# Last layer of a four-layer gated graph network: the state copied beneath the edge sums, part of the low h moved, the new state behind the n gate's argument

## The reference

```python
for l in range(4):
    m = x @ weight[l]
    agg = segment_sum(m[src], dst, num_segments=50000)
    gi = agg @ w_ih.T + b_ih              # i_r, i_z, i_n
    gh = x @ w_hh.T + b_hh                # h_r, h_z, h_n
    r = sigmoid(i_r + h_r); z = sigmoid(i_z + h_z)
    n = tanh(i_n + r * h_n)
    x = (1 - z) * n + z * x
return layernorm(input + (x + input), eps=1e-5)
```

## Time and profile before

| | |
|---|---|
| Median of three runs | 2331.55 us (2330.46 to 2332.36) |
| Span of the profiled execution (first to last instruction) | 2327.4 us |
| Busy in the span | TensorE 96%, VectorE 93%, ScalarE 79%, GpSimd 74% |
| Granted TensorE clock, mean | 0.986 |

### The profile page before, as it was taken

How to read it: one execution, slowest core, us unless ns; L and a number is a source line. 1 busy time by engine, 2 the same in 40 slices (tenths; PEclk the granted TensorE clock), 3 DMA queues, 4 the chain that set the end, 5 groups by cost and what they waited for, 6 DMA issues and landing times.

```text
span 2327.4 us, 49180 instructions
## 1 busy us (share of the span) xinstructions
PE 2229.5 (96%) x11728; PEld 1898.3 (82%) x11728; DVE 2175.6 (93%) x4211; ACT 1842.3 (79%) x3483; POOL 1719.4 (74%) x1654
## 2 busy tenths in 40 slices
PE   3999999999999999999999999999989999999996
PEld 2888888888878888888878888888877888888885
DVE  7899999999879999999969999999969999999998
ACT  1688888888768888888857888888856888888886
POOL 3877777777487777777558777777748888888884
PEclk7999999999999999999999999999999999999998
DMA  2455555555545555555545555555544555555554
GB/s 58 120 155 160 158 160 161 158 160 160 157 131 173 171 173 172 174 172 173 166 127 172 172 171 172 173 174 171 174 130 122 159 156 155 155 155 154 155 155 118
DMA packets 277064, 362.45 MB, mean 156 GB/s; under 512 B 107754, under 2 KB 186586, under 8 KB 276980
## 3 DMA queue, kind: packets, MB, share of 16 engines
q1 hardware_dynamic: 238118, 309.12, 43.5%
q0 software_dynamic: 38784, 52.30, 9.7%
q10 hardware_dynamic: 78, 0.08, 0.0%
HBM read 208.71 MB, written 179.20 MB: 167 GB/s over the span
## 4 chain that ended last, share of the span: by engine, by line
PE 66%; DVE 18%; issue 10%; ACT 2%; DMA 2%; POOL 1%; DVEq 1%; SPq 0%; ACTq 0%; POOLq 0%
PE pZ L847 17%; PE pR L847 8%; PE pHN L847 8%; PE pA L835 8%; PE pO L929 5%; PE pIN L847 4%; PE pA L847 4%; DVE bn L1442 3%; PE pR L891 3%; PE pR L888 3%; PE pR L889 3%; DVE diff L1411 3%; DVE aggT L1381 3%; DVE y_rows L1435 2%; PE pH L786 2%
## 5 line engine op out<-in xcount | busy, mean ns | idle before, releaser
L683 POOL DMA_INDIRECT gath<-state,idx x900 | 931.4, 1035 | 264.6 <-issue 255.8
L660 POOL TENSOR_TENSOR h_lo<-hT,h_hi 128x500 fp32r<-128x500 f32 (+1 forms) x400 | 375.8, 940 | 200.5 <-ACT h_hi L1050 149.7
L683 POOL DMA_INDIRECT gath<-in_x_dram,idx x300 | 321.9, 1073 | 101.8 <-issue 68.7
L1080 ACT ACTIVATE rg<-pR,bsum 128x500 f32<-128x500 f32 x400 | 269.7, 674 | 112.2 <-PE pR L891 100.2
L1400 DVE SCALAR_TENSOR_TENSOR narg<-pHN,bhh,rg 128x500 f32<-128x500 f32 x400 | 292.3, 731 | 44.9 <-ACT rg L1080 44.1
L1372 DVE TENSOR_TENSOR a_lo<-aggT,a_hi 128x500 fp32r<-128x500 f32 x396 | 271.5, 686 | 0.3
L1062 ACT CAST sel<-sel 128x504 fp32r (+1 forms) x400 | 245.9, 615 | 31.6 <-DVE flag_i L1356 29.5
L1417 DVE TENSOR_TENSOR diff<-pZ,diff 128x500 f32<-128x500 f32 x400 | 267.7, 669 | 0.8
L1381 DVE TENSOR_TENSOR aggT<-pA,hT 128x500 f32<-128x500 f32 x396 | 263.8, 666 | 1.7 <-PE pA L835 1.6
L1088 ACT ACTIVATE pZ<-pZ,bsum 128x500 f32<-128x500 f32 x400 | 256.1, 640 | 0.0
L1067 ACT CAST a_hi<-aggT 128x500 fp32r<-128x500 f32 x396 | 235.6, 595 | 6.5 <-DVE aggT L1381 6.5
(11 more groups left out here) (211 smaller groups left out, 6384.1 us busy)
## 6 DMA issues: line engine op xcount, KB each, us to landing
columns<-newT SPq DMA_DIRECT2D x300, 250.0 KB, 2.3
hT<-columns SPq DMA_DIRECT2D x300, 250.0 KB, 2.7
state<-o_rows SPq DMA_DIRECT2D x300, 224.0 KB
x_rows<-in_x_dram SPq DMA_DIRECT2D x200, 224.0 KB
out_dram<-o_rows SPq DMA_DIRECT2D x91, 224.0 KB
gath<-state,idx POOLq DMA_INDIRECT x900, 2.4
state<-o_rows SPq DMA_DIRECT2D x297, 26.0 KB
idx<-edge_src SPq DMA_DIRECT2D x395, 1.5 KB
```

Of the source, the lines that this page charges most:

```text
L660: nc.gpsimd.tensor_tensor(part_of(h_lo, u)[:, cols], hT[:, u % RING, cols], part_of(h_hi, u)[:, cols].bitcast(F32), ALU.subtract).then_inc ...
L683: pool.indirect_dma_start(out=gath[:, u % RING, j, :], out_offset=None, in_=states[l], in_offset=bass.IndirectOffsetOnAxis(ap=idx[:, u % R ...
L1080: nc.scalar.activation(rg[:, :], pR[:, 0:COLS], ACT.Sigmoid, bias=bsum[:, 0:1]).then_inc(s_r, 1)
```

## The change

Only the last layer changes (in the diff: constants and the two tests, GpSimd, TensorE, ScalarE, VectorE). From block 6 on, ScalarE copies the state `hT` of block b+2 into the sums' place in `pA` (`state_beneath_sums`, at the head of its step b, ahead of the r gate of b), and TensorE adds the edge sums onto it: its matmuls begin without clearing. VectorE's `aggregate` is left out for these blocks, and `a_hi` and `a_lo` are taken from `pA` itself. The copy waits until `a_lo` of the block before (b+1) is made; the edge sums wait for the copy. For blocks whose number modulo five is 1 or 2 (from block 7 on), VectorE makes the whole `h_lo` (`low_h`, ahead of `a_lo` in its step) and GpSimd doesn't. And VectorE's `renew` of block b-1 stands behind the n gate's argument of b instead of ahead of it.

```diff
+BENEATH = 6
+BY_VECTOR = 1, 2
+        def beneath(l, i, u):
+            return l == L - 1 and not (isinstance(i, int) and i == 0 and u < BENEATH)
+        def by_vector(l, i, u):
+            return l == L - 1 and u % RING in BY_VECTOR and not (isinstance(i, int) and i == 0 and u < RING + BY_VECTOR[1])
...
-                        if coming:
+                        if coming and not by_vector(coming[0], coming[3], coming[2]):
                             split_h(*coming[:3], l * NB + b if exists_before(i, u, 1) else None)
...
-                at_least(s_agg, g, start)
+                if onto:
+                    pe.wait_ge(s_beneath, UNROLL * i + u - BENEATH + 1)
+                else:
+                    at_least(s_agg, g, start)
...
+                    if onto or (spreading and k):
+                        begins = False
...
+            def state_beneath_sums(l, i, u):
+                b = UNROLL * i + u
+                if isinstance(b, int) and b == BENEATH:
+                    act.wait_ge(s_agg, l * NB + b)
+                else:
+                    act.wait_ge(s_alo, l * NB + b)
+                act.wait_ge(s_load[u % RING], 16 * (TURNS * (l - 1) + turn(i, u) + 1))
+                nc.scalar.copy(sums_of, by_rows(hT[:, u % RING, :])).then_inc(s_beneath, 1)
...
+                        if final and not ramp and exists(i, u, 2):
+                            state_beneath_sums(l, *after(i, u, 2)[:0:-1])
                         r_gate(l, b, u, first and l == 0)
...
-                            high_part(l, *after(i, u, 2)[:2])
+                            high_part(l, *after(i, u, 2)[:2], beneath(l, *after(i, u, 2)[:0:-1]))
...
                         r_times_hn(l, b, u)
                         if shifted:
                             shift(*shifted)
-                        if not ramp and not last:
+                        if not ramp and not last and not final:
                             renew(*after(i, u, -1))
                         n_argument(l, b, u)
+                        if not ramp and not last and final:
+                            renew(*after(i, u, -1))
...
-                        if summed and not (ramp and u == 3):
+                        if summed and not (ramp and u == 3) and not under:
                             aggregate(l, *summed)
...
-                        coming = coming if coming and halved(coming[0]) else None
+                        coming = coming if coming and (halved(coming[0]) or by_vector(coming[0], coming[3], coming[2])) else None
                         if coming and not ramp and not last:
                             low_h(*coming[:3])
                         if summed and not (ramp and u == 3):
-                            low_part(l, *summed)
+                            low_part(l, *summed, under)
```

More of the change, by code:

```diff
@@ L315, in build @@
         s_pA = sem("edges_summed")
+        s_beneath = sem("state_copied_beneath_sums")
         s_agg = sem("agg_made")
@@ L385, in halved, with low_counts @@
             return 0 < l < L - 1
+        def beneath(l, i, u):
+            return l == L - 1 and not (isinstance(i, int) and i == 0 and u < BENEATH)
+        def by_vector(l, i, u):
+            return l == L - 1 and u % RING in BY_VECTOR and not (isinstance(i, int) and i == 0 and u < RING + BY_VECTOR[1])
+        def low_counts(l, i, u):
+            if l < L - 1:
+                return l * NB + UNROLL * i + u + 1, (l - 1) * NB + UNROLL * i + u + 1 if l else None
+            first = sum(by_vector(l, 0, v) for v in range(UNROLL if not (isinstance(i, int) and i == 0) else u + 1))
+            if isinstance(i, int) and i == 0:
+                return l * NB + u + 1 - first, 2 * NB + first if first else None
+            group = sum(by_vector(l, 1, v) for v in range(UNROLL))
+            mine = sum(by_vector(l, 1, v) for v in range(u + 1))
+            return (l * NB + UNROLL - first + (UNROLL - group) * (i - 1) + u + 1 - mine,
+                    2 * NB + first + group * (i - 1) + mine)
         def unsplit(l, b):
@@ L820, in sum_edges @@
                 g = l * NB + b
-                at_least(s_agg, g, start)
+                onto = beneath(l, i, u)
+                spreading = l == L - 1 and isinstance(b, int) and b == BENEATH - 1
+                if onto:
+                    pe.wait_ge(s_beneath, UNROLL * i + u - BENEATH + 1)
+                else:
+                    at_least(s_agg, g, start)
                 pe.wait_ge(s_sel, g + 1)
@@ L834, in sum_edges @@
                     ends = not begins or unsplit(l, b)
-                    last = nc.tensor.matmul(to, rows, cols, start=begins, stop=ends)
+                    if onto or (spreading and k):
+                        begins = False
+                    last = nc.tensor.matmul(to, rows, cols, start=begins, stop=ends, skip_group_check=onto or spreading)
                 last.then_inc(s_pA, 1)
@@ L849, in product, with r_on_state @@
                 return last
-            def r_on_state(l, b, u, start, halves, ready=1):
+            def r_on_state(l, b, u, start, by_pool, by_dve=None):
                 g = l * NB + b
-                pe.wait_ge(s_hlo, g + ready)
-                if halves:
-                    pe.wait_ge(s_hlov, g + 1 - NB)
+                pe.wait_ge(s_hlo, by_pool)
+                if by_dve is not None:
+                    pe.wait_ge(s_hlov, by_dve)
                 at_least(s_r, g, start)
@@ L938, in step @@
                         ramp = isinstance(i, int) and i == 0 and u < RAMP
-                        r_on_state(l, b, u, start, halved(l))
+                        r_on_state(l, b, u, start, *low_counts(l, i, u))
                         if not start:
@@ L1001, in one @@
                         last.then_inc(s_pA, 1)
-                        r_on_state(l, b, 0, start, False, PRE + 1)
+                        r_on_state(l, b, 0, start, l * NB + b + PRE + 1)
                         hn_on_state(l, b, 0, start)
@@ L1364, in low_h @@
                 dve.wait_ge(s_hhi, l * NB + b + 1)
-                v.tensor_tensor(part_of(h_lo, u)[:, HALF:COLS], hT[:, u % RING, HALF:COLS],
-                                part_of(h_hi, u)[:, HALF:COLS].bitcast(F32), ALU.subtract).then_inc(s_hlov, 1)
+                cols = slice(HALF if halved(l) else 0, COLS)
+                v.tensor_tensor(part_of(h_lo, u)[:, cols], hT[:, u % RING, cols],
+                                part_of(h_hi, u)[:, cols].bitcast(F32), ALU.subtract).then_inc(s_hlov, 1)
             def low_part(l, b, u, summed=False):
@@ L1517, in step @@
                         summed = after(i, u, 1 if ramp else 2)[:2] if exists(i, u, 2) else None
-                        if summed and not (ramp and u == 3):
+                        under = bool(summed) and not ramp and beneath(l, *after(i, u, 2)[:0:-1])
+                        if summed and not (ramp and u == 3) and not under:
                             aggregate(l, *summed)
```

## The result

| | before | after |
|---|---|---|
| Median of the runs | 2331.95 us (2330.46 to 2332.75, 4 runs) | 2390.07 us (2388.57 to 2393.48, 4 runs) |
| Span of the profiled execution | 2327.4 us | 2388.3 us |

The ratio is 1.0252, with a 95% interval of 1.024 to 1.0265: slower by 58 us, where 63.4 us were forecast (2395; range 2373 to 2414).

A forecast was written before the change was run, and what follows sets the result against it. VectorE was taken to bound the kernel at 5.65 us a plain step; the new loop through ScalarE makes 6.14. Longer steps +45.6, low h +21.8 and small terms gave +63.4 us: 2395 us, range 2373 to 2414.

The forecast's parts named there:

- The loop through ScalarE: Last layer, `a_lo` to copy to r gate to r times hn: plain step 6.14 us against 5.65, 6.73 with low h.
- the copy's hold on ScalarE: Time from the copy's start to the r gate's on ScalarE: taken as 0.57 us, bounds 0.50 to 0.68.
- VectorE's idle time: VectorE, waiting for the r gate ahead of r times hn: idles some 0.87 us a step.
- The sum: Whole last layer: longer steps +45.6, low h +21.8, small instructions -3.8, two steps without copy -0.39 + 0.19; together +63.4 us.
- From the span to the median: Whole kernel: 4.15 us between profiled span and median of the runs, added to a span of about 2391.
- `a_lo` from PSUM: VectorE's `a_lo` reading `pA`: no change from 0.67 us, though the skill's 62 extra cycles would add 6 us in all.
- The second loop: `newT`, TensorE's transposes and products, r gate, next step's r times hn: 5.69 us, 0.45 shorter than ScalarE's loop, costs nothing.
- GpSimd's relief at nothing: GpSimd loses low h, 37 times 1.2 us; nothing on the loop waits for it, so no gain.
- Rival 1: Last layer: only the loop through TensorE's transposes decides; plain steps 5.69 us, low h 5.85, about 2335; chance 6%.
- rival 2: Last layer: neither loop holds, VectorE's work decides; faster, 2316, or 2312 to 2320 with small instructions; chance 5%.
- rival 3: TensorE, no longer full, drops to 1.2 GHz: +470 us, 2800; chance 1%.
- rival 4: ScalarE's copy: a wrong count lets it wait for an older `a_lo`; chance counted inside the 5% of rival 2.

The follow-up runs named there:

- two single edits: Kernel before with only the new state moved behind the n gate's argument: 2351.37 us; with only low h moved to VectorE for two of five blocks: 2351.51 us.
- the early order: The change with copy, `a_hi` and `a_lo` placed earlier and the new state back ahead of the n gate's argument, same instructions: 2309.06 us, ratio 0.9906.

## Why the prediction was right

- *VectorE sets the step before.* Right: each of two single edits that only lengthen VectorE's own row of instructions cost what they add to it (+19 and +20 us for 18 and 21.8).
- *The loop through ScalarE.* Right in every piece but one: `a_lo` starts 4.10 us after r times hn (4.08), the copy 0.04 after its end, r times hn 0.12 after the r gate's end (0.10). The term that was off is the copy's hold on ScalarE: 0.51 and not 0.57. The n gate with its bias pointer, which I took as one end of the range, was the wrong row to lean on; whether the pointer is the reason no run shows. The estimate of 0.51 from the figures of the Trainium skill ("ScalarE: Activation LUTs", What ACT_TABLE_LOAD costs) was the better one. The trace agrees with it: 0.51 to the next start, and a copy of 0.58 us where the same figures give an estimated 0.60.
- *VectorE's idle time.* It shows as 0.75 us in a plain step, where about 0.9 was given as the sign. The 0.87 was counted from the point at which the next instruction could have started, and the profile counts from the end of the product.
- *The sum.* With 6.11 - 5.65 = 0.46 in place of 0.49 in 93 steps, the 63.4 us become 60.6. That the two profiled spans lie 60.9 apart is closer than it deserves, and in part luck: block 4's r times hn, ahead of which the two kernels do the same, starts 1.95 us later in the trace after (1756.48 and 1754.53). From there to block 98's the trace takes 604.49 us after (to 2360.97) and 545.44 before (to 2299.97), 59.1 more. Most of what is left lies in one step, block 9's, which took 6.82 us in the kernel before, where the same place of the later groups takes 5.75 to 5.78.
- *From the span to the median.* The 4.15 us are not what lies around the first and the last instruction. In the runs that have both on record a run's time is 1.7 to 2.1 us above its own span (2390.14 and 2388.3 after), so the profiled execution before was some 2.4 us faster than the median of its runs. Of the 4.9 us between 2395 and 2390 these are about a half.
- *The range.* Its ends, added up from the bounds given, leave out those of low h: with 37 x (0.71 - 0.59) = 4 the upper one is 2419 and not 2415. Nothing hangs on it.
- *`a_lo` from PSUM.* 0.67 us as before (medians 0.672 and 0.673), so reading PSUM adds nothing here. The surcharge that the prediction worked out from the Trainium skill ("VectorE: DVE Perf Modes", The TRN2 errata), an estimated 0.065 us, does not show in this trace.
- *Sums that add to what stands in `pA`.* The prediction left their cost open. Where they don't wait, the six edge sums of a block last 1.02 us, in the kernel before (2003.94) and in the early order (2012.35) alike.
- *The second loop.* It is there but slack: TensorE's transposes wait for the new state in the profile, and the run with the new state ahead won only VectorE's 0.19 us a step. The estimate of 0.45 us of slack was 0.19 too large: the first loop is 0.03 shorter than worked out, and this one takes 5.85 us and not 5.69, mainly because the transposes start 0.13 us after the new state's end, not 0.05, and where they waited the next product follows them by 0.45, not 0.35.
- *GpSimd's relief at nothing.* Right for the change (67.5 us of waiting in the stretch) and for the kernel before (+20 us by moving low h alone). That GpSimd has a floor 0.3 us under VectorE's five steps I hadn't seen; it decides only when the steps get shorter than in either kernel.
- *The rivals.* Rival 1 asked for the r gate to be released by TensorE, rival 2 for VectorE without idle time, rival 3 for a lower clock: the waits, the timeline and the windows show none of these. For rival 4 the copy would have to start without regard to `a_lo` of block b+1, and it waits for it in each of the 62 steps.

## What to carry to other kernels

Here, taking work from the full engine helped only once the instruction that took its place no longer waited for something that the full engine makes late. Before moving work, walk once round each loop that the new wait closes, in the written order of every engine, and compare the sum with the step. Where the loop is too long, look first for the instruction on it that could stand earlier: here the same work in another order turned 58 us lost into 22 won.

## What the runs showed of the hardware

- Two neighbours on VectorE of which the second needs the first's result start further apart: r times hn and the n gate's argument 0.84 us in place of 0.65, `diff` and the product 0.77 in place of 0.57. With an instruction of 128x500 between them nothing is lost; with the small shift of 0.18 us between them the argument still starts 0.84 behind r times hn (2272.04 and 2272.88 in the change). Over 95 steps the first pair alone cost some 18 of 19 us.
- A ScalarE copy of 128x500 float32 from SBUF to PSUM lasts 0.58 us and holds the next instruction for 0.51; the cast `a_hi` lasts 0.57 when it reads PSUM (after) and 0.59 when it reads SBUF (before).
- TensorE's first edge sum starts 0.23 us after the copy's end (2010.42 + 0.58, 2011.23), twice the 0.12 that VectorE takes to follow ScalarE's r gate.
